# Expert weights in one tensor per 128-column piece, their addresses computed ahead of each tile, on one Trainium2 core

## The reference

```python
x = L0_attn_x                                   # [8, 512, 128] fp32
x = x + 0.5 * _L0_ffn_ref(_layernorm(x), ...)   # 24 experts, width 512, top 2
x = x + _L0_attn_ref(_layernorm(x), ...)        # linear attention, 16 heads
x = x + 0.5 * _L0_ffn_ref(_layernorm(x), ...)
x = x + 0.5 * _L1_ffn_ref(_layernorm(x), ...)   # 8 experts, width 256, top 2, and a shared one
x = x + _L1_attn_ref(_layernorm(x), ...)        # causal attention, rotary
x = x + 0.5 * _L1_ffn_ref(_layernorm(x), ...)

def body(acc, expert):                          # one expert of _L0_ffn_ref
    h = jax.nn.gelu(xf @ w1e + b1e, approximate=False)
    y = h @ w2e + b2e
    return (acc + ce[:, None] * y, None)
```

## Time and profile before

| | us |
|---|---|
| median of 3 runs (lowest to highest) | 1033.47 (1031.43 to 1034.35) |
| the profiled execution's own time | 1034.46 |
| its span in the profile | 1033.1 |
| TensorE busy | 903.7 (87%) |
| VectorE busy | 563.8 (55%) |
| ScalarE busy | 476.0 (46%) |
| GpSimd busy | 493.5 (48%) |

### The profile page before, as it was taken

The page is one execution under the profiler, slowest core; times in us unless marked ns, Lnnn a source line. Parts: engine busy times, 40 slices in busy tenths (PEclk is TensorE's granted clock), DMA queues, the critical chain, the costliest instruction groups (busy, mean ns, idle before and its releaser), DMA issues.

```text
span 1033.1 us, 25972 instructions
## 1 busy us (share of the span) xinstructions
PE 903.7 (87%) x8524; PEld 786.1 (76%) x8524; DVE 563.8 (55%) x2208; ACT 476.0 (46%) x804; POOL 493.5 (48%) x519
## 2 busy tenths in 40 slices
PE   4478999998999599999899999996999999999860
PEld 2237999986899577899898898983778878778850
DVE  6785800055787065785038500588793988874022
ACT  3224454348654358645345444452538354454320
POOL 0551047073015771007474561776744447477765
PEclk9768999999999899999999999998999999999995
DMA  9946764452352543363452356832633143436772
GB/s 317 385 148 175 214 142 104 96 116 47 63 113 81 121 83 76 54 173 101 114 121 65 90 125 137 164 83 66 112 103 100 53 100 88 100 97 157 159 162 74
DMA packets 219623, 126.02 MB, mean 122 GB/s; under 512 B 137456, under 2 KB 199792, under 8 KB 219248
## 3 DMA queue, kind: packets, MB, share of 16 engines
q1 hardware_dynamic: 203120, 90.77, 37.2%
q0 software_dynamic: 16384, 33.59, 11.8%
HBM read 40.13 MB, written 56.90 MB: 94 GB/s over the span
## 4 chain that ended last, share of the span: by engine, by line
PE 57%; DVE 16%; POOL 9%; DMA 7%; issue 7%; ACT 4%; SPq 0%; POOLq 0%; ACTq 0%; DVEq 0%
PE bank L1530 21%; PE bank L1506 6%; PE bank L1508 5%; PE bank L1507 5%; POOL rows L2214 5%; POOL got L2234 4%; PE bank L1392 3%; DMA got<-y_l,slot_index 3%; PE bank L1345 2%; DMA turned<-rows 2%; PE bank L1528 2%; PE bank L1321 2%; PE bank L1364 2%; DVE x_res L2030 2%; PE bank L1402 2%
## 5 line engine op out<-in xcount | busy, mean ns | idle before, releaser
L1530 PE MATMUL bank<-blocks_l,hid 128*128 x2496 | 361.5, 287 | 0.0
L2214 POOL DMA_INDIRECT rows<-rows_sent,slot_index x192 | 186.3, 970 | 325.5 <-issue 248.3
L2234 POOL DMA_INDIRECT got<-y_l,slot_index x256 | 243.8, 953 | 188.9 <-PE bank L1530 74.5
L1530 PEld LDWEIGHTS bank<-blocks_l,hid 128*128 128x128 f32 x2496 | 312.1, 192 | 6.3 <-issue 1.3
L1678 ACT ACTIVATE hid<-bank 128x512 f32<-128x512 f32 (+1 forms) x316 | 185.2, 592 | 262.0 <-PE bank L1508 255.4
L1506 PE MATMUL bank<-turned,blocks_l 128*128 128x128 f16 x1248 | 238.9, 224 | 41.5 <-DMA turned<-rows 25.6
L2030 DVE SCALAR_TENSOR_TENSOR x_res<-got,share,x_res 128x128 f32<-128x128 f32 x256 | 78.2, 348 | 321.8 <-DMA got<-y_l,slot_index 319.4
L1508 PE MATMUL bank<-turned,blocks_l 128*128 128x128 f16 x1248 | 238.8, 224 | 0.0
L1507 PE MATMUL bank<-turned,blocks_l 128*128 128x128 f16 x1248 | 237.5, 223 | 0.0
L1506 PEld LDWEIGHTS bank<-turned,blocks_l 128*128 x1248 | 125.7, 101 | 56.2 <-issue 51.5
L1507 PEld LDWEIGHTS bank<-turned,blocks_l 128*128 x1248 | 124.6, 100 | 4.1 <-issue 1.3
(11 more groups left out here) (209 smaller groups left out, 1230.0 us busy)
## 6 DMA issues: line engine op xcount, KB each, us to landing
y_l<-y SPq DMA_DIRECT2D x92, 256.0 KB
blocks_l<-in_w_dram SPq DMA_DIRECT2D x4, 1536.0 KB, 17.1
got<-in_w_dram SPq DMA_DIRECT2D x16, 256.0 KB, 6.5
got<-y_l,slot_index POOLq DMA_INDIRECT x256
rows<-own SPq DMA_DIRECT2D x1, 3584.0 KB, 14.5
rows<-own SPq DMA_DIRECT2D x7, 512.0 KB, 4.1
hid<-in_w_dram SPq DMA_DIRECT2D x12, 256.0 KB, 5.3
rows<-rows_sent,slot_index POOLq DMA_INDIRECT x192, 2.7
```

What stands on the lines that cost most here:

```text
L1530: m = t.do.matmul(out, hid[:, j * H + c * P:j * H + c * P + P], second[:, at], start=False, stop=(c == C - 1))
L2214: d = g.do.indirect_dma_start(rows_dram[s], at, rows[:, 2 * D * i:2 * D * i + 2 * D], None)
L2234: d = g.do.indirect_dma_start(got_mem[slot][:, col:col + D], None, y_dram[layer][s][layer.team(ev.i)], at)
```

## The change

Each layer's weights become one tensor per 128-column chunk and half, with the experts side by side at 128 columns: `first_high`, `first_low` (fp16) and `second` (fp32), and a small `select` tensor. The register now holds the expert's number. Ahead of a tile's matmuls, all addresses that they will need are asked for at once; the matmuls use the same expressions, so that nothing is computed again.

```diff
+        firsts = {layer: [cuts(layer, "first_high"), cuts(layer, "first_low")] for layer in LAYERS}
+        seconds = {layer: [cuts(layer, "second_high"), cuts(layer, "second_low")] if layer.terms else [cuts(layer, "second", F32)] for layer in LAYERS}
...
+            def cut_of(mem, e):
+                return mem[:, :].rearrange("p (e h) -> p e h", h=P)[:, bass.ds(e, 1), :].rearrange("p e h -> p (e h)")
+            def address(e, name, size, columns, last):
+                nc.lower_val(e * columns * size + (sb_at[name] + last * size), [TENSOR])
+            def first_addresses(layer, e):
+                for c in range(layer.chunks):
+                    for half in ("high", "low"):
+                        address(e, f"first_{half}_{layer.name}_{c}", 2, P, P - 1)
...
-                    high, low, _, _ = block_parts(block_for(ev, j), H)
-                    for c, at in enumerate(spans(C)):
+                    e, (high, low) = expert_of(ev, j), firsts[layer]
+                    first_addresses(layer, e)
+                    for c in range(C):
                         out = hb[:, j * H + c * P:j * H + c * P + P]
-                        t.do.matmul(out, high[:, at], xh, start=True, stop=False)
+                        t.do.matmul(out, cut_of(high[c], e), xh, start=True, stop=False)
```

```diff
+                for i in range(BT):
+                    root, minus_mean = sm[:, 2 * BT + i:2 * BT + i + 1], sm[:, 3 * BT + i:3 * BT + i + 1]
+                    m = a.do.activation(xn[:, D * i:D * i + D], x[:, BT * ev.i + i, :], ACT.Identity, bias=minus_mean, scale=root)
```

```diff
-EARLIER = {(VE, "norm_g"): 3, (PE, "ca_v"): 0.5, (VE, "r_soft"): -4, (SC, "ystore"): 0.5, (PE, "ca_out"): -3, (SC, "l1"): -4, ...
+EARLIER = {(VE, "add"): -4, (VE, "norm_a"): -1, (PE, "ca_out"): 0.5, (SC, "split_1"): -3, (PE, "turn_a"): -3, (VE, "norm_g"): 1, ...
```

More of the change, by code:

```diff
@@ L57, in __init__ @@
         self.groups = self.tiles // BT
-        self.block = 2 * hidden + 4
+        self.parts = experts // PART_EXPERTS
     def team(self, b):
@@ L491, in second @@
         def second(ev):
+            if not LAYERS[int(ev.kind[3:])].terms:
+                if ev.kind == "w2_0":
+                    yield Await([split_of(W1_PARTS[0][W2_AFTER * ev.i])])
+                yield from self.stage(*ev)
+                self.mark(split_of(ev))
+                return
+            raw = self.raw[int(ev.kind[3:])]
+            yield Take(raw, [ev], 1)
             yield from self.stage(*ev)
-            self.mark(ev)
+            yield from self.stage("upper" + ev.kind[2:], 0, 0, ev.i)
+            yield from self.stage("halve" + ev.kind[2:], 0, 0, ev.i, {PE: lambda: self.give(raw, ev)})
+            self.mark(split_of(ev))
         def selects():
@@ L776, in second @@
             yield Await(["halved"])
+            if layer.terms:
+                yield Take(self.hid, [l1], 1)
+                yield from self.stage("hid", s, p, unit, {VE: lambda: self.give(self.banks, (l1, 0))})
             yield Await([("l1", s, p, min(unit + FIRSTS_AHEAD, units[-1]))])
@@ L965, in macaron_program, with buffers @@
         xn_mem, xt_mem = slots("xn", 2), slots("xt", 2)
-        parked = blocks[L1][:, 0:len(PARKED_SETS) * EARLY_BUFFERS * SEQ].rearrange("p (i n c) -> p i n c", n=EARLY_BUFFERS, c=SEQ)
+        def buffers(mem):
+            words = mem[:, :] if mem.dtype == F32 else mem[:, :].bitcast(F32)
+            return [words[:, at:at + SEQ] for at in range(0, words.shape[1], SEQ)]
+        parked = [buffer for mem in pieces[L1] for buffer in buffers(mem)]
+        late = [buffer for mem in pieces[L0][:-2] for buffer in buffers(mem)]
@@ L980, in macaron_program @@
+        assert len(late) >= 6 * LATE_SETS + 2 * LATE_ROWS
+        late_weights, late_const = (mem[:, :].bitcast(F32)[:, 0:n] for mem, n in zip(pieces[L0][-2:], (WCOLS - WEIGHTS_KEPT, CCOLS - CONST_KEPT)))
         rows_all = sb("rows_sent", [P, ROW_BUFFERS, SEQ], F32)
@@ L1004, in macaron_program @@
         heads_dram = [nc.dram_tensor(f"heads{i}", [HEADS, D, SEQ // HEADS], F32, kind="Internal").ap() for i in range(BATCHES)]
-        blocks_dram = nc.dram_tensor("blocks_parked", [P, L1.E * L1.block], F32, kind="Internal").ap()
+        pieces_dram = [nc.dram_tensor(f"parked{n}", list(mem.shape), mem.dtype, kind="Internal").ap() for n, mem in enumerate(pieces[L1])]
         def wcol(name):
@@ L1054, in set_of @@
             i = pool.at[user]
-            return [mem[i][:, n, :] for n in range(mem[i].shape[1])], small[i]
+            return mem[i], small[i]
         def xn_of(role, ev):
@@ L1227, in bank_read @@
             if kind == "l1":
-                return hidden_gelu[s].after(ev)
+                return hidden_low[s].after(Ev("hid", *ev[1:])) if LAYER[ev.p].terms else hidden_gelu[s].after(ev)
             if kind == "out":
```

338 lines of the change are left out of this document (227 added, 111 removed).

## The result

The changed kernel takes 1043.52 us (median of 4 runs, 1041.48 to 1045.36); the kernel before took 1032.45 us in the same comparison (4 runs, 1031.26 to 1034.35). The ratio is 1.0101, with a 95% interval of 1.008 to 1.0122: slower by some 10 us, where I forecast 1007. That is beyond the 3.1 us that I took for noise, though within 2%. The profiled execution took 1045.4 us, with a span of 1044.0.

What follows compares the result with a forecast made beforehand. The prediction took TensorE as the bound, with a few holes and a GpSimd-paced end. Its terms, -17 - 8 + 2 - 2 - 3.7 + 2 = -26.7 us, took 1034.5 to 1007.8 (median 1007), range 994 to 1028.

Steps and rivals of the forecast that it cites:

- The wait at 346 us: TensorE idle 10.39 us before stream 0's round 1; rank 8.4 us earlier, so -8 us, ends 0 and -10.4.
- the same place in stream 1: Stream 1's round 1: more tiles ahead of its ranks, so the wait grows by +2 us, ends 0 and +7.
- the start: Up to the first expert matmul: 6 us later, but 8 us of work done ahead; -2 us, ends -8 and +6.
- the end: GpSimd's last list: the 3.67 us hole before 1008.22 us closes; -3.7 us, ends 0 and -3.7.
- the register operations: Gaps before TensorE's expert matmuls, 22.5 us in 450 places, go; less restarts and longer waits, -17 us.
- the norm: ScalarE instead of VectorE places 40 batches, lengthening chains but relieving VectorE; +2 us, ends -6 and +8.
- put at nothing: Same weight bytes in other pieces, six parking transfers for one, the `select` placing, the register load: no effect counted.
- the premise: Whole kernel: TensorE sets the pace, with a few holes, a start of 86 us and a GpSimd-paced end.
- my second rival: Other engines take up TensorE's gain; half the register and 346 us terms becomes waiting, about 1020 us; chance 0.15.
- Steps at 0.056 us, at most 24 restarts: Sign of being right: steps into expert matmuls at 0.056 us nearly everywhere, with at most some 24 restarts.
- First expert near 92: Sign of being right: TensorE's first expert matmul comes near 92 us, against 86.16 us before.
- The slower rival: ScalarE's queue: norm placings wait for VectorE and hold gelus, each delaying TensorE 1 us; +40, 1047 us; chance 0.10.

Runs made afterwards that it cites:

- e2: Changed kernel with VectorE instead of ScalarE placing the normalised batches, every engine's order kept: 1043.8 us, ratio 1.010 to the kernel before.
- e1: Changed kernel's tensors and addresses asked together, but VectorE placing the norm and the planner's shifts and costs of before: 1019.4 us, ratio 0.985 to the kernel before.
- e13: Kernel of e1 run again as a base for e14 to e16 on the same chip: 1018.8 us, ratio 0.986 to the kernel before.
- e16: Kernel of e5 (e1 without asking for addresses ahead) run again beside e13: 1020.3 us, ratio 0.988 to the kernel before.
- e5: e1 without its calls that ask for addresses ahead, all orders those of e1: 1019.9 us, ratio 0.991 to the kernel before.
- e4: Changed kernel without its two calls that ask for a tile's addresses ahead of the matmuls: 1044.6 us, ratio 1.011 to the kernel before.
- e15: e1 with one fp16 matmul fewer in every tile, 22.6 us less of TensorE: 1007.8 us, ratio 0.976 to the kernel before.
- e14: e1 with one fp16 matmul more in every tile, 22.6 us more of TensorE: 1022.7 us, ratio 0.990 to the kernel before.
- e6: e1 with ScalarE placing the forty batches, other engines' orders as in e1: 1025.4 us, ratio 0.994 to the kernel before.
- e9 to e12: Four runs on e1 or the changed tensors: a matmul added, one taken, planner tables switched at 640 us, and the reverse: ratios 1.000, 0.983, 0.994, 1.024.
- e9: e1 with the first fp16 matmul of every tile made twice, beside a kernel before that took 1200.25 us: 1200.0 us, ratio 1.000.

## Why the prediction was wrong

**By its size, the step that failed is the order, which I summed at four places only.** The wait at 346 us (-8), the same place in stream 1 (+2), the start (-2) and the end (-3.7) make -12 together. The order as a whole costs +24 to +25: that is e2 against e1 or e13, which run the same instructions in another order. These 37 us are the whole distance from 1007 to 1043.5. What is left of my sum, -17 for the register operations and +2 for the norm, is -15, and e1 is 15 us faster than before. The lists behind 640 us, where some 16 of the 25 us are lost, stand in none of my terms, not even among those put at nothing: I looked at the end of GpSimd's list, and the swap of gather and scatter stands ahead of it.

**By its mechanism, the premise failed too.** I wrote that the kernel "is a TensorE program with a few holes", from the slices and from 57% of the chain, and took 17 us for 22.5 us of gaps. At a fixed order asking ahead, which ends 14.6 us of gaps, is worth 1.5 us (e16 against e13; 6 by the ratios of e5 and e1), and nothing that can be measured in the changed order (e4). So that e1's 15 us match my -17 is in good part luck. TensorE is busy for 87% of the span but passes on only part of what it gains: of 22.6 us of matmuls half when they are taken out (e15), a sixth when they are put in (e14). From e16 to e13 its waits for rows and batches grow by 11 us, since they end when GpSimd's and VectorE's chains end. That was my second rival, for which I had taken half off; for asking ahead most goes. The rule of the Trainium skill (Advanced Engine Details and Errata, Engine Queue Depths and Sequencer Loop), by which I said the term would be zero, comes near the size of what asking ahead is worth. The trace does not bear out its reason: register operations do stand as gaps, 15.1 us of them in e16.

Point by point:

- *Steps at 0.056 us, at most 24 restarts:* right, 12 gaps up to 904 us.
- *A fused operation between 46 and 92 ns:* 74, right.
- *Wait at 346 us down to 2:* 3.6, near; its -8 wrong. The 5 tiles are gone from ahead of the rank, but 6.5 us of what they free becomes waiting ahead of it. Only -1.4 arrived.
- *Waits for `turned` over 22 us, the sign of the second rival:* 25.9 us.
- *Stream 1, rank at 479.3, scatter at 487.6:* 480.5 and 487.1, right, and the first expert comes 1.9 us later for my +2.
- *First expert near 92:* 100.7, wrong; I had not counted a wait for weights, nor that the splits behind it run at the 1.2 GHz level. As forecast, work done ahead pays it back. e1, with before's shifts, has it at 91.3.
- *End:* the hole is gone, right, and hides nothing of the 14 us by which the list starts late. The last gather, forecast 23 us or more earlier, comes 10.9 us later.
- *Norm on ScalarE:* I bounded an ACTIVATE by 290 to 450 ns and took +2 us (what I took off VectorE, 40 * 1.2, is 48 us and not 50). It is 483 ns, over the bound; the estimate from the Trainium skill (ScalarE: Activation LUTs, What ACT_TABLE_LOAD costs), some 480 ns, agrees. It costs 9 us in e1's order (e6), outside my ends by a little, and none in the changed one (e2).
- *The slower rival, 1047, placings that hold gelus:* its time is near the result, its mechanism is not: without the placings (e2) the time is the same, and in the changed kernel no wait of TensorE for `hid` is over 0.4 us.

What the other edits of the change bring can be told only in sum. e1 is 15 us faster than before (14.4 in e13), asking ahead is 1.5 to 6 of it. The rest lies in the smaller tensors, whose addresses are mostly one plain add (gaps of 15.1 us instead of 22.5), in the splits and in 25 stages moved at the start: in e16's profile the end of stream 0's first round is 6 us earlier, that of stream 1's second 12, the whole 13. Which of the three it is I didn't try.

## What to carry to other kernels

In a program of several engines with an order made by a planner, a new cost or a new table can be the largest part of a change: here the order cost 24 us, and the new tensors, addresses and start together brought 15. So test an edit with the order frozen, and compare the whole lists of every engine, not only their ends: look for a step that heads the chain of the last work and has moved behind one that nobody waits for. An engine that is busy for 87% of the span is not the bound until a dose of work, added to and taken from it, shows in the time one for one.

## What I had not expected of the hardware

- Register operations leave gaps in the matmuls even as plain adds of 32 ns: e16 has 274 gaps with 15.1 us, 0.055 us each, and about half of these us stand ahead of a plain add.
- TensorE's granted clock moves with small changes: with 14.6 us fewer gaps (e13) the mean over five runs is 0.950, with them 0.955, with a matmul more per tile 0.960, with one fewer 0.948. In the profiles of e13 and e16 that goes with 66 and 37 us of work at the 1.2 GHz level, which may be part of why the gaps' end brings so little.
- The same kernel took 1200 us beside e9 to e12 and 1027 to 1037 elsewhere, with TensorE waiting on "issue" in many places (e9). There the ratio of the same two kernels was 1.024 instead of 1.042 for the one and 0.994 both times for the other: a ratio taken where everything is slower needs its own base.
